# Sums of squares of keys and queries: as rows in four column tiles, turned back by a selection, instead of one-column matmuls

## What is computed

```python
q = _short_conv(hidden_states @ Wq.T, conv_q).reshape(b, l, H, DK)
k = _short_conv(hidden_states @ Wk.T, conv_k).reshape(b, l, H, DK)
v_direct = _short_conv(hidden_states @ Wv.T, conv_v).reshape(b, l, H, DV)
beta = jax.nn.sigmoid(hidden_states @ Wb.T)
...
def _l2norm(x):
    return x * jax.lax.rsqrt(jnp.sum(x * x, -1, keepdims=True) + 1e-06)
...
q = _l2norm(q)
k = _l2norm(k)
v = v * beta[..., None]
kb = k * beta[..., None]
```

## Time and profile before

| | us |
|---|---|
| median of 3 runs | 501.77 |
| the runs | 503.24, 496.82, 501.77 |
| profiled execution, its own time | 497.99 |
| profiled execution, span from first to last instruction | 496.1 |

### The profile page before, as it was taken

One profiled execution on the slowest core, in us unless ns is written; L12 is line 12 of the kernel. 1 busy time (PEld: TensorE's weight loads), 2 busy tenths in 40 slices (PEclk: granted clock), 3 DMA queues, 4 the chain that ended last, 5 costly groups with the idle time before them and its releaser, 6 DMA issues.

```text
span 496.1 us, 8167 instructions
## 1 busy us (share of the span) xinstructions
PE 440.6 (89%) x3172; PEld 301.2 (61%) x3172; DVE 320.7 (65%) x602; ACT 160.9 (32%) x202; POOL 76.8 (15%) x79
## 2 busy tenths in 40 slices
PE   1997997899969897999999499996998899999994
PEld 1862333455555565658785298885445688888861
DVE  5542145466982899998757974701313999999945
ACT  1102111244730010112225060003004788788630
POOL 1000000000004390001563100371000000000070
PEclk9999999899987887999989859999999999999998
DMA  8999909633040415006400200287006999999543
GB/s 322 431 424 429 419 16 317 215 80 90 1 169 1 104 75 145 23 1 261 167 3 0 87 0 1 64 277 231 2 0 253 378 411 366 419 373 420 216 131 123
DMA packets 17937, 92.33 MB, mean 186 GB/s; under 512 B 3424, under 2 KB 5104, under 8 KB 10736
## 3 DMA queue, kind: packets, MB, share of 16 engines
q1 hardware_dynamic: 14880, 78.74, 42.1%
q10 hardware_dynamic: 1488, 8.93, 5.1%
q0 software_dynamic: 1536, 4.20, 2.5%
HBM read 82.17 MB, written 12.08 MB: 190 GB/s over the span
## 4 chain that ended last, share of the span: by engine, by line
PE 73%; DVE 19%; issue 3%; another core or an unknown queue 2%; ACT 1%; DMA 1%; SPq 0%; DVEq 0%; ACTq 0%
PE bank L805 29%; PE bank L645 7%; PE bank L586 5%; PE bank L613 5%; PE bank L490 3%; PE bank L520 3%; PE bank L541 3%; DVE part L1305 3%; PE bank L500 3%; DVE ring L1305 3%; PE bank L629 1%; PE bank L775 1%; PE bank L793 1%; DVE x L1471 1%
## 5 line engine op out<-in xcount | busy, mean ns | idle before, releaser
L586 PE MATMUL bank<-xnT,ring 128*128 128x512 f32 x96 | 44.6, 618 | 0.7 <-ACT xnT L944 0.7
L1305 DVE SCALAR_TENSOR_TENSOR part<-ring,cols,part 128x504 f32<-128x504 f32 (+13 forms) x64 | 43.9, 748 | 0.1
L645 PEld LDWEIGHTS bank<-ring 64*64 64x64 f32 x960 | 34.2, 144 | 10.0 <-issue 9.1
L645 PE MATMUL bank<-ring 64*64 64x64 f32 (+1 forms) x960 | 38.4, 235 | 1.8 <-issue 1.6
L413 POOL TENSOR_TENSOR small<-small 128x1 f32<-128x1 f32 (+1 forms) x13 | 12.1, 930 | 160.0 <-DVE small L1192 94.4
L1305 DVE SCALAR_TENSOR_TENSOR ring<-bank,cols,ring 128x504 f32<-128x504 f32 (+2 forms) x36 | 26.4, 734 | 15.8 <-ACT ring L991 14.8
L613 PE MATMUL bank<-early,ring 128*32 128x512 f32 (+15 forms) x512 | 34.2, 413 | 0.0
L586 PEld LDWEIGHTS bank<-xnT,ring 128*128 128x128 f32 x96 | 18.3, 196 | 21.7 <-issue 20.7
L476 PE MATMUL bank<-consts,part 128*128 128x128 f32 x48 | 11.0, 381 | 20.9 <-DVE part L1198 14.0
L1089 ACT ACTIVATE rows<-bank 128x512 f32<-128x512 f32 x19 | 11.4, 598 | 49.0 <-PE bank L805 28.1
L613 PEld LDWEIGHTS bank<-early,ring 128*32 128x32 f32 x512 | 14.2, 113 | 15.7 <-issue 11.8
(11 more groups left out here) (228 smaller groups left out, 943.3 us busy)
## 6 DMA issues: line engine op xcount, KB each, us to landing
early<-wffn_in SPq DMA_DIRECT2D x21, 1024.0 KB, 7.9
ring<-ctxT_in SPq DMA_DIRECT2D x4, 2048.0 KB, 27.2
ring<-ctx_in SPq DMA_DIRECT2D x4, 2048.0 KB, 31.6
raw1b<-wffn_in SPq DMA_DIRECT2D x6, 1024.0 KB
raw3b<-wffn_in SPq DMA_DIRECT2D x6, 1024.0 KB, 7.1
raw2b<-wffn_in SPq DMA_DIRECT2D x6, 1024.0 KB, 8.4
ring<-firw_in SPq DMA_DIRECT2D x4, 1024.0 KB, 5.7
xs<-zeros_in ACTq DMA_DIRECT2D x1, 3840.0 KB, 14.0
```

Of the source, the lines that this page charges most:

```text
L586: last = pe.matmul(bank[5 + g % 3][:, :], wqkv[:, j, c, h * P:(h + 1) * P], xnT[:, c, :], start=(c == 0), stop=(c == DC - 1))
L645: last = pe.matmul(dst[s, d], left[s, L * t:L * (t + 1)], right(s, t), start=True, stop=True)
L1305: return dve.scalar_tensor_tensor(out=d, in0=s, scalar=w, in1=d, op0=ALU.mult, op1=ALU.add)
```

## The change

Instead of eight groups of four one-column matmuls there are two blocks, for k and for q. The squares of four heads are kept (in `att`, a buffer of the attention matrices that is free then). `sum_rows(k)` is four matmuls, one per head, whose stationary operand is a column of ones repeated to 32 columns and whose moving operand is the plane of squares over all 512 tokens; each writes 32 equal rows into the 32 partitions of bank 4 that belong to its column tile. ScalarE copies the bank into `sum_row` (`keep_sums`). `turn_sums(k)` is four matmuls, one per tile of 128 tokens, with a piece of `sum_row` as stationary operand and every 32nd column of the identity as moving one, so that one row of each head is selected and comes out as a column; the results stand in columns 0 to 31 of bank 2. The first block stands behind g=9 and its turn behind g=10; the second block and turn stand behind the transposes of v. In ScalarE's queue `keep_sums(0)` stands between SiLU and square of g=8, `keep_sums(1)` behind the last square. The semaphores `ct_done` and `ct_ready` are merged with the new ones.

```diff
--- before.py
+++ after.py
@@ -138,12 +138,14 @@
         oT_b = early[:, 2, 0:1024].rearrange("p (i n) -> p i n", i=2)
         o_b = early[:, 2, 1024:2048].rearrange("p (i n) -> p i n", i=2)
         bgrow, bgprod = o_b[:, 0, :], o_b[:, 1, :]
-        sq_b = early[:, 2, 1024:2048].rearrange("p (i n) -> p i n", i=2)
+        sum_row = early[:, 2, 1024:1536]
         flat = ring[:, :, :].rearrange("p t n -> p (t n)")
         wqkv = flat[:, 0:6144].rearrange("p (j c n) -> p j c n", j=3, c=DC)
         wod = flat[:, 6144:8192].rearrange("p (h n) -> p h n", h=H)
         vP, kP, qP, kbP, lt01, lt23, ttlt, att, tmmt, uP, bv = (
             flat[:, 8192 + 2048 * i:8192 + 2048 * (i + 1)].rearrange("p (h n) -> p h n", h=H) for i in range(11))
+
+        sq_b = att
 
         def compact(block, i):
             return block.rearrange("p h n -> p (h n)")[:, 1024 * i:1024 * (i + 1)].rearrange("p (h n) -> p h n", h=H)
@@ -240,7 +242,7 @@
                  "s_done", "bias_ready", "exp_done", "pT_done", "pT_ready",
                  "oT_done", "oT_ready", "proj_done", "x1_done", "gate_done", "gate_read", "gate_exp_wanted",
                  "gate_exp_done", "qkv_done", "lag0_done", "conv_done", "silu_done", "sq_done", "sumsq_done",
-                 "vt_done", "bv_ready", "cc_ready", "ct_done", "ct_ready", "kq_done", "kq_ready", "kk_done",
+                 "vt_done", "bv_ready", "cc_ready", "cols_done", "cols_kept", "kq_done", "kq_ready", "kk_done",
                  "mt_ready", "at_done", "at_ready", "tt1_ready", "t1_done", "t1_ready", "lt_ready", "yl_done",
                  "yl_ready", "zz_done", "t_upd", "tt_upd", "u_done", "u_ready", "o_done",
                  "bc_done", "weighted", "summed", "o_ready", "osq_ready", "osum_done", "m_done", "x2_done", "rout_done",
@@ -337,7 +339,7 @@
             build_stack(3)
             load_firw(3)
             sp.wait_ge(S["fir_done"], H)
-            sp.wait_ge(S["sumsq_done"], 2 * H)
+            sp.wait_ge(S["sumsq_done"], 2)
 
             def load_shared(which, e):
                 sp.dma_start(raws[which][e][:, :] if e else raws[which][e],
@@ -571,11 +573,20 @@
 
             pe.wait_ge(ld_wqkv, 16)
 
-            def sumsq(i):
-                pe.wait_ge(S["sq_done"], i + 1)
+            def sum_rows(k):
+
+                pe.wait_ge(S["sq_done"], H * (k + 1))
+                for i in range(H):
+                    last = pe.matmul(bank[4][CG * i:CG * (i + 1), :], ones[:, 0:1].broadcast_to([P, CG]), sq_b[:, i, :],
+                                     start=True, stop=True)
+                last.then_inc(S["cols_done"], 1)
+
+            def turn_sums(k):
+
+                pe.wait_ge(S["cols_kept"], k + 1)
                 for t in range(NT):
-                    last = pe.matmul(bank[4][:, 256 + NT * i + t:257 + NT * i + t], sq_b[:, i % 2, t * P:(t + 1) * P],
-                                     ones[:, 0:1], start=True, stop=True)
+                    last = pe.matmul(bank[2][:, 16 * k + t:16 * (k + 1):NT], sum_row[:, t * P:(t + 1) * P],
+                                     ident[:, 0:P:CG], start=True, stop=True)
                 last.then_inc(S["sumsq_done"], 1)
 
             for g in range(3 * H):
@@ -588,8 +599,10 @@
                 last.then_inc(S["qkv_done"], 1)
                 if g == H:
                     gate_logits()
-                if g >= H + 2:
-                    sumsq(g - H - 2)
+                if g == 2 * H + 1:
+                    sum_rows(0)
+                if g == 2 * H + 2:
+                    turn_sums(0)
             for h in range(H):
                 pe.wait_ge(S["silu_done"], h + 1)
                 if h >= 2:
@@ -597,8 +610,8 @@
                 for t in range(NT):
                     last = pe.transpose(bank[h % 2][:, t * P:(t + 1) * P], vP[:, h, t * P:(t + 1) * P], ident)
                 last.then_inc(S["vt_done"], 1)
-            sumsq(2 * H - 2)
-            sumsq(2 * H - 1)
+            sum_rows(1)
+            turn_sums(1)
 
             def fir_rounds(h, lo, hi):
 
@@ -619,7 +632,7 @@
             pe.wait_ge(S["cc_ready"], 1)
             for t in range(NT):
                 last = pe.transpose(bank[3][0:24, t * P:(t + 1) * P], cc[:, t, :], ident)
-            last.then_inc(S["ct_done"], 1)
+            last.then_inc(S["cols_done"], 1)
             pe.wait_ge(S["ct_lo"], 1)
 
             def spread(dst, row):
@@ -991,6 +1004,11 @@
                 act.activation(plane[j][:, h], bank[5 + g % 3][:, :], ACT.Copy,
                                scale=cols[:, w:w + 1]).then_inc(S["lag0_done"], 1)
 
+            def keep_sums(k):
+
+                act.wait_ge(S["cols_done"], k + 1)
+                act.activation(sum_row, bank[4][:, :], ACT.Copy).then_inc(S["cols_kept"], 1)
+
             def silu(g):
                 j, h = g // H, g % H
                 act.wait_ge(S["conv_done"], g + 1)
@@ -998,9 +1016,9 @@
                 if j > 0:
                     i = g - H
                     act.wait_ge(S["silu_done"], g + 1)
-                    if i >= 2:
-                        act.wait_ge(S["sumsq_done"], i - 1)
-                    act.activation(sq_b[:, i % 2, :], plane[j][:, h], ACT.Square).then_inc(S["sq_done"], 1)
+                    if i == H:
+                        keep_sums(0)
+                    act.activation(sq_b[:, i % H, :], plane[j][:, h], ACT.Square).then_inc(S["sq_done"], 1)
 
             lag0(0)
             for g in range(1, 3 * H):
@@ -1009,6 +1027,7 @@
                 if g in (H + 2, H + 3):
                     gate_exp(g - H - 1)
             silu(3 * H - 1)
+            keep_sums(1)
 
             def keep_fir(h):
 
@@ -1017,8 +1036,8 @@
 
             act.wait_ge(S["xT_done"], 2 * NT)
             keep_fir(0)
-            act.wait_ge(S["ct_done"], 1)
-            act.activation(ct[:, 0, :], bank[3][0:24, :], ACT.Copy).then_inc(S["ct_ready"], 1)
+            act.wait_ge(S["cols_done"], 3)
+            act.activation(ct[:, 0, :], bank[3][0:24, :], ACT.Copy).then_inc(S["cols_kept"], 1)
             keep_fir(1)
             for h in range(H):
                 act.wait_ge(S["t1_done"], h + 1)
@@ -1352,8 +1371,8 @@
                 dve.tensor_tensor(bv[:, h].rearrange("p (t n) -> p t n", t=NT),
                                   bank[h % 2][:, :].rearrange("p (t n) -> p t n", t=NT),
                                   beta[:, :, h:h + 1].broadcast_to([P, NT, P]), ALU.mult).then_inc(S["bv_ready"], 1)
-            dve.wait_ge(S["sumsq_done"], 2 * H)
-            after(dve, dve.tensor_scalar(rs_in[:, 0:32], bank[4][:, 256:288], 1e-6, None, ALU.add), S["pow_wanted"])
+            dve.wait_ge(S["sumsq_done"], 2)
+            after(dve, dve.tensor_scalar(rs_in[:, 0:32], bank[2][:, 0:32], 1e-6, None, ALU.add), S["pow_wanted"])
             clear_heads(1)
             rsqrt(ktr, 0, 32)
             ktr3 = ktr.rearrange("p (i t) -> p t i", t=NT)
@@ -1367,7 +1386,7 @@
                     ins.then_inc(S["cc_ready"], 1)
             for h in range(H):
                 if h == 0:
-                    dve.wait_ge(S["ct_ready"], 1)
+                    dve.wait_ge(S["cols_kept"], 3)
                     dve.tensor_tensor(ct[:, 1, :], bank[3][0:24, :], ct[:, 0, :].bitcast(F32),
                                       ALU.subtract).then_inc(S["ct_lo"], 1)
                 dve.wait_ge(S["kq_done"], h + 1)
```

## The result

| | before, us | changed, us |
|---|---|---|
| median, 20 executions each | 501.29 | 505.50 |
| lowest and highest | 496.82, 505.92 | 501.23, 507.34 |
| mean | 501.05 | 504.83 |
| profiled execution, its own time | 497.99 | 507.31 |
| span of the profiled execution | 496.1 | 505.5 |

The ratio is 1.0086, with a 95% interval of 1.0055 to 1.0118: 2.8 to 5.9 us slower. The ratios leave out executions more than 1.5% above the fastest of their kernel in the same group of runs, so they can differ from the means where the fastest is a rare one (as in the group of e9 to e12, where before has 494.06 once). By 2% this counts as the same.

A forecast was written before the change was run, and what follows sets the result against it. The prediction took VectorE's chain to bound the loop (worth 0) and TensorE the stage's end (+1.05 us). Added to a base of 500.0 us, this gave 501.0 us, range 497.5 to 505.0.

The forecast's parts named there:

- The loop's chain and its slack: Groups 6 to 11: VectorE's chain runs without a wait, new waits leave 1.7 to 2.0 us to spare; worth 0.
- TensorE's relief: Loop: TensorE saves 3.6 us, forecast not to reach the end; rival that it counts, 497.4 us, chance 0.05.
- The end's sum: Behind the transposes of v: block, copy and turn take 4.25 us in place of 3.20, so +1.05 us.
- The rows of the block ran side by side: Forecast for the block's column tiles, 1.72 us at the end; rival that they don't, 507.0 us, chance 0.03.
- The Trainium skill's rule on the drain: At the end, each of two tiling-mode changes would cost 0.2 us, making the sum +1.5 us; left at 0.
- It goes into both of what hangs on it: End of stage: the added 1.05 us delays both the FIR in TensorE's queue and the power in VectorE's.
- so the 1.05 us pass through: Behind the end's sums: the chain goes on through the table's copy, so the whole 1.05 us reaches the time.
- The clock falls in the loop: Rival: clock halves for 10 us at TensorE's idle ahead of the loop's block; +3.7, 503.7 us, chance 0.08.
- the row it was weighed by: Ahead of 40.66 us: a 1.90 us wait between full-size matmuls left the clock at 1.00, taken as evidence against a fall.
- the 2.65 that were worked out: VectorE's waits for lag-0 copies if the clock falls in the loop: +1.15 us at g=10, +1.5 at g=11.
- the 0.02 for what was not thought of: Chance of 0.02 kept for unlisted causes, as four executions of the same kernel differ by 6 us.
- The base: Mean of the four known times of the kernel before, 500.0 us, to which the term was added.

The follow-up runs named there:

- e9: The kernel before plus seven small VectorE instructions (about 1.5 us) at about 280 us; mean 501.44 us, +0.3 +-1.1 against before.
- e12: The kernel before with one of the two last sums of squares moved into TensorE's idle time ahead of the last transposes; mean 499.42 us, -1.8 +-1.3 against before.
- e3: The kernel before with one more one-column sum of squares at the end of the stage; mean 502.24 us, -0.2 +-0.7 against before.
- e2: The change in the loop only, for the keys; queries by one-column sums, two at the end as before; mean 505.48 us, +3.0 +-0.6 against before.
- e13: The change in the loop only, plus seven small VectorE instructions (1.5 us) at about 280 us; mean 505.80 us, +2.6 +-0.7 against before.
- e10: The changed kernel plus seven small VectorE instructions (about 1.5 us) at about 280 us; mean 502.08 us, against 504.83 for the changed kernel beside it.
- e17: The changed kernel plus seven small VectorE instructions (1.5 us) at about 280 us, on another chip; mean 505.85 us, against 509.56 for the changed kernel.
- e1: The change at the end of the stage only, for the queries; keys by one-column sums in the loop as before; mean 504.06 us, +1.6 +-0.9 against before.
- e14: The changed kernel with the router's ranking matmuls split by the dense group that stood behind them; mean 506.28 us, +3.1 +-0.8 against before.
- e6: The kernel before with four unread dense matmuls in TensorE's idle time ahead of the last transposes of v; mean 503.04 us, -0.5 +-0.7 against before.

## Why the prediction was wrong

Point by point, by its own steps.

- The loop's chain and its slack: right. It is VectorE's without a wait in the changed kernel's first profile, with 2.3 and 1.7 us to spare, and the clock stayed at 1.00 there. TensorE's relief did not come through.
- The end's sum: right in its make-up, 0.2 us too small: 4.45 us in place of 4.25, of which the block has 0.19. The rows of the block ran side by side: 8 records in 1.91 us, where one behind the other would be 6.9. The Trainium skill's rule on the drain ("TensorEngine Tiling (Array Packing)", section "Key Properties") would have added 0.4 by the estimate made there; no run takes it apart from the rest, so it stays neither shown nor excluded.
- "It goes into both of what hangs on it" and "so the 1.05 us pass through": the first step that failed. It took the FIR's 9.11 us as fixed. The FIR took 10.33, with 2.5 us more of it at half clock, so 2.35 us came out of the stage in place of 1.05. In e3 it was 9.89, in e12 9.96. And what comes out of the stage does not pass through as it is: e3 has the same 2.4 us more and a mean of -0.2 +-0.7.
- "The clock falls in the loop": the row it was weighed by was misleading. The wait of 1.90 us that left the clock at 1.00 in the earlier trace rows was followed by half clock in the changed kernel's profile, where nothing is changed yet:

```profile
40.02 5.35 PE L522 MATMUL bank<-ring,early 128*64 128x512 f32 x16 [1.89 <-ACT early L977]
```

  16 records take 5.35 us in place of 3.65. One execution shows what can happen after such a wait, not what will. The rival itself did not come true in the changed kernel. Only e2 and e13 showed a fall in the loop, behind the sum that they add there, with VectorE waiting 0.99 us in each and not the 2.65 that were worked out.
- The sum was made as if all outside of the stage stayed as it is. The clock's levels behind the stage stand at nothing in it, without a reason; only the 0.02 for what was not thought of covers them. This is the step that made the forecast wrong. 0.01 of mean clock goes with 4 us, the changed kernel's executions lie 0.0083 lower in one group (0.9268 against 0.9351) and 0.0066 in the other (0.9253 against 0.9319), and most of its loss goes with that. A part of it is made in the stage and in the FIR. Another part, 3 us by e10 and e17, is made where the program meets the clock's levels 150 us later, and 1.5 us more of work there took it away.
- The base was the mean of four times, 500.0. The median of 20 executions is 501.29, so 1.3 of the 4.5 us between forecast and result are the base's, and 3.2 the term's. That the forecast had the right sign is worth little: its 1.05 us are the stage's alone, and a stage lengthened as much in e3 gave no loss.
- The range ended at 505.0, half a microsecond short. It held the spread of before's executions, but no case in which the whole spread moves up.

What stays open: why the changed kernel's profiles have more half clock late in the program than those of before and e3, although e3's stage is as long. The end alone (e1, none of it from 310 to 400 us in its profile) costs less than the whole, e2 costs nearly as much but has a fall of its own, and e14, which changed the late place itself, did not gain. The runs show that one late shift takes the loss away, on two chips. They don't show which part of the change brings it, nor a rule by which the place could be foretold.

## What to carry to other kernels

Where TensorE's clock moves between its two levels, the time of a kernel is not the sum of its stages: a stage made 2.3 us shorter (e6) or 2.4 us longer (e3) moved the mean by less than the measurement tells, and 1.5 us of added work lowered it by 3 us (e10, e17). So compare means over many executions with the granted clock of each beside its time, and put the same small late shift into both kernels before you lay a difference of under 1% on the edit itself. And a block that frees TensorE on a stretch where another engine is the chain buys nothing in its stage, while each hop that it adds at the stretch's end, where nothing covers, lengthens the stage (4.45 us in place of 3.20 here).

## What was not expected of the hardware

Executions of the same kernel on the same chip spread over 10 us, and its time went with the mean granted clock at 3.96 us per 0.01. A wait of 1.90 us of TensorE was followed by full clock in one execution and by half clock in another. Dense matmuls directly behind the 8-column ones of the ranking ran at half clock (5.47 us for 12 records) in the changed kernel's profile and at full clock (3.01 us) in the profile of before. VectorE stood still for 12 to 14 us while GpSimd issued its indirect DMAs in all four profiled executions on one chip, and in none of the four on another.
